# A recurrent gated-memory kernel: GpSimd takes quarter 0's product and half of each cell's hidden rows, under a new order on every engine

## What is computed

```python
encoded = tanh(xt @ We + st @ Ue + be)                                   # 24 values
new_state = tanh(einsum('bd,cds->bcs', xt, Wx) + einsum('bs,cst->bct', st, Ws) + bk)   # 8 candidates of 32
mem = concatenate([[encoded, err]], mem[:-1])                            # the last 20 entries
a = relu(mem.reshape(b, -1) @ enc_w1 + enc_b1)
agent_in = relu(a @ enc_w2 + enc_b2)
h1, c1 = lstm_cell(agent_in, h1, c1, ...)
h2, c2 = lstm_cell(h1, h2, c2, ...)
gate = softmax(h2 @ gate_w + gate_b)
theta = clamp01(mean(abs(mem[:, :10, -1])) * 2.5)
gate = gate * theta + gs * (1 - theta)
st = einsum('bc,bcs->bs', gate, new_state)
pred = clamp01(st[:, -1]); err = pred - yt
```

## Time and profile before

| | us |
|---|---|
| median of 3 runs | 5656.6 (5656.21 to 5656.87) |
| span of the profiled execution | 5654.1 |
| busy: PE, DVE, ACT, POOL | 5444.6, 4678.1, 3830.9, 1646.7 |
| instructions: PE, DVE, ACT, POOL | 67584, 12841, 9217, 3589 |
| DMA, mean | 30 GB/s |

### The profile page before, as it was taken

How to read it: one execution, slowest core, us unless ns; L and a number is a source line. 1 busy time by engine, 2 the same in 40 slices (tenths; PEclk the granted TensorE clock), 3 DMA queues, 4 the chain that set the end, 5 groups by cost and what they waited for, 6 DMA issues and landing times.

```text
span 5654.1 us, 184300 instructions
## 1 busy us (share of the span) xinstructions
PE 5444.6 (96%) x67584; PEld 3397.7 (60%) x67584; DVE 4678.1 (83%) x12841; ACT 3830.9 (68%) x9217; POOL 1646.7 (29%) x3589
## 2 busy tenths in 40 slices
PE   7999999999999999999999999999999999999998
PEld 4666666666666666666666666666666666666665
DVE  7888888888888888888888888888888888888887
ACT  5666666666666666666666666666666666666665
POOL 2222222222222222222222222222222222222222
PEclk9999999999999999999999999999999999999999
DMA  2111111111111111111111111111111111111111
GB/s 66 28 29 30 28 31 28 31 28 31 28 31 28 31 28 28 31 28 31 28 31 28 31 28 31 28 29 30 28 31 28 31 28 31 28 31 28 31 28 39
DMA packets 299286, 172.38 MB, mean 30 GB/s; under 512 B 156734, under 2 KB 263882, under 8 KB 298714
## 3 DMA queue, kind: packets, MB, share of 16 engines
q1 hardware_dynamic: 293568, 159.42, 10.8%
q10 hardware_dynamic: 5146, 3.66, 0.2%
HBM read 74.65 MB, written 2.10 MB: 14 GB/s over the span
## 4 chain that ended last, share of the span: by engine, by line
PE 69%; ACT 15%; DVE 12%; issue 4%; DMA 0%; POOL 0%; ACTq 0%; POOLq 0%; DVEq 0%
PE chain L412 17%; PE a_ps L374 10%; PE cand_ps L343 8%; PE cand_ps L334 8%; ACT a_sb L523 6%; PE chain L399 6%; PE a_ps L363 6%; ACT gates L548 5%; DVE cell_in L708 5%; DVE added L694 4%; PE chain L308 4%; PE a_ps L385 4%; PE chain L429 4%; PE cand_ps L329 3%; ACT tanh_c L554 3%
## 5 line engine op out<-in xcount | busy, mean ns | idle before, releaser
L363 PE MATMUL a_ps<-hist,w_hist 125*64 125x512 f16 x12288 | 1700.2, 381 | 24.9 <-DMA w_hist<-enc_table 24.9
L785 DVE TENSOR_REDUCE state<-mixed 128x64 f32<-128x512 f32 x2048 | 1352.6, 681 | 34.1 <-POOL mixed L873 0.7
L541 ACT ACTIVATE cand<-cand_ps 128x512 f32<-128x512 f32 x2048 | 1154.6, 590 | 184.8 <-PE cand_ps L343 184.8
L412 PE MATMUL chain<-cell_in,cell_w 128*64 128x128 f32 x16384 | 1092.8, 276 | 0.7 <-ACT cell_in L531 0.5
L412 PEld LDWEIGHTS chain<-cell_in,cell_w 128*64 128x64 f32 x16384 | 888.3, 136 | 288.2 <-ACT cell_in L531 181.5
L900 POOL TENSOR_TENSOR err_ring<-pred_now,ys 128x8 f32 x512 | 128.6, 251 | 3106.0 <-DVE pred_now L792 3106.0
L548 ACT ACTIVATE gates<-chain 128x512 f32<-128x512 f32 x1024 | 611.4, 597 | 619.8 <-PE chain L412 619.8
L363 PEld LDWEIGHTS a_ps<-hist,w_hist 125*64 125x64 f16 x12288 | 658.6, 110 | 447.2 <-issue 26.0
L554 ACT ACTIVATE tanh_c<-gates 128x128 f32<-128x128 f32 x1024 | 316.7, 309 | 690.0 <-DVE gates L700 690.0
L694 DVE SCALAR_TENSOR_TENSOR added<-gates 128x256 f32<-128x256 f32 x1024 | 435.5, 425 | 419.4 <-ACT gates L548 419.4
L708 DVE SCALAR_TENSOR_TENSOR cell_in<-gates,tanh_c 64x128 f32<-64x128 f32 x2048 | 588.0, 287 | 159.4 <-ACT tanh_c L554 145.6
(11 more groups left out here) (74 smaller groups left out, 6660.7 us busy)
## 6 DMA issues: line engine op xcount, KB each, us to landing
x_sb<-in_x_l SPq DMA_DIRECT2D x260, 256.0 KB, 2.8
hist<-entry_parts SPq DMA_DIRECT2D x2048, 25.0 KB
w_hist<-enc_table SPq DMA_DIRECT2D x258, 128.0 KB, 2.4
y_rows<-in_y_l SPq DMA_DIRECT2D x260, 8.0 KB
ys<-in_y ACTq DMA_DIRECT2D x1, 2048.0 KB, 16.3
preds_out<-preds SPq DMA_DIRECT2D x1, 2048.0 KB, 8.1
cand<-in_encoder ACTq DMA_DIRECT2D x1, 640.0 KB, 3.8
cell_w<-in_cell ACTq DMA_DIRECT2D x2, 256.0 KB, 4.8
```

Source lines behind the costliest of these rows:

```text
L363: nc.tensor.matmul(a_ps[g][ENC * half:ENC * half + ENC, :], w_hist[0:HROWS, w_slot(u), kk, wp, :], hist[0:HROWS, xp, k, at:at + 512], star ...
L412: last = nc.tensor.matmul(chain[g][rows, P * r:P * r + P], cell_w[c][:, hf, r, :], cell_in[c][:, g, hf, :], start=False, stop=True, skip_g ...
L541: ins = nc.scalar.activation(cand[:, g, q // 2, :, q % 2, :, :].rearrange("p h s c -> p h (s c)"), cand_ps[q][:, :].rearrange("p (h k) -> ...
L785: V.tensor_reduce(state[:, g, hf, 2 * pair:2 * pair + 2, :], mixed[:, pair, hf, :, :, :], AX, ALU.add)\
```

## The change

What it does:

- **GpSimd forms quarter 0's product too.** `mix(pair 0)` is no longer called on VectorE; `mix_quarter` is called for q = 0 and q = 1, each with its own semaphore (`q_mulpool[q]`).
- **Half of each cell's new hidden rows goes to GpSimd**, in two instructions: `out_gate_low` adds 1 to the output gate in 64 rows as soon as the gates are there, and `new_hidden` on GpSimd multiplies with the value's tanh. VectorE keeps the other 64 rows in one instruction. `cell_gates` and `gate_logits` wait for both (`q_h`, `q_h_pool`), and `next_hidden` on ScalarE waits for each half.
- **A semaphore for each sum**: `q_sum[hf][pair]`, waited for one by one.
- **History in one-pass pieces**: `history(item, kk, first, end)` issues single passes, which the new order lays between the other work of TensorE. One of the twelve passes is issued in the item's first phase and eleven in its second.
- **A new order on all compute engines**, and `candidates_x` split in `candidates_bias` (one item ahead) and `candidates_x`. The second encoder layer, the cells and the gate logits of an item are now in its third phase (`old`). `keep_prediction` gets a wait of its own.

The diff, without comments on it and cut to its core:

```diff
-SUMS = 2
-CAND_ORDER = (2, 1, 3, 0)
-MIX_ORDER = (1, 0)
+CAND_ORDER = (3, 2, 1, 0)
+POOL_HALF = (0, 1)
+PIECES = ((0, 0), (1, 0), (0, 1))
...
             def state_transpose(item, hf):
                 g, n, u = item
-                pe.wait_ge(q_sum[hf], SUMS * n)
+                for pair in range(2):
+                    pe.wait_ge(q_sum[hf][pair], n)
...
-            def encoded_x(item, before, extra):
+            def encoded_x(item, extra):
                 g, n, u = item
                 x_wait(item, extra)
-                if before:
-                    for pair in MIX_ORDER:
-                        pe.wait_ge(q_mul[pair], before[1] + GROUPS if pair == MIX_ORDER[1] else before[1])
+                pe.wait_ge(q_mul[1], n)
...
+            def candidates_bias(item):
+                g, n, u = item
+                for q in CAND_ORDER:
+                    pe.wait_ge(q_cand[q], n)
                 for q in range(Q):
                     rows = slice(D_IN * q, D_IN * q + D_IN)
                     nc.tensor.matmul(cand_ps[q][:, :], ones16[rows, :], cand_bias[rows, :],
                                      start=True, stop=False, skip_group_check=True)
...
-            def history(item, kk):
+            def history(item, kk, first=0, end=len(PIECES)):
                 g, n, u = item
                 k = HT - 1 - kk
-                for t, (wp, xp) in enumerate(((0, 0), (1, 0), (0, 1))):
+                for t in range(first, end):
+                    wp, xp = PIECES[t]
...
                     pe.wait_ge(q_h[0], n)
+                    pe.wait_ge(q_h_pool[0], n)
...
                 pe.wait_ge(q_h[1], n)
+                pe.wait_ge(q_h_pool[1], n)
...
 # TensorE, the new order
+                if old:
+                    bias_of_cell(old, 0)
+                    encoder2(old)
+                    candidates_x(old)
+                    cell_gates(old, 0)
+                    candidates_s(old)
+                if cur:
+                    history(cur, 0, 1, 2)
+                if old:
+                    bias_of_cell(old, 1)
+                if cur:
+                    history(cur, 0, 2, 3)
+                    history(cur, 1, 0, 1)
+                    encoded_x(cur, extra)
+                    history(cur, 1, 1, 2)
+                if old:
+                    cell_gates(old, 1)
+                if cur:
+                    history(cur, 1, 2, 3)
+                    state_transpose(cur, 0)
+                    state_transpose(cur, 1)
+                    history(cur, 2, 0, 1)
+                if old:
+                    logit_bias(old)
+                if cur:
+                    history(cur, 2, 1, 2)
                     encoded_s(cur)
+                    history(cur, 2, 2, 3)
                     history(cur, 3)
                 if old:
                     gate_logits(old)
                 if cur:
                     encoder1_now(cur)
                 if new:
+                    history_waits(new, extra)
+                    history(new, 0, 0, 1)
+                if cur:
+                    candidates_bias(cur)
...
 # ScalarE, the new order
+                if cur:
+                    at_least_zero(cur)
+                    encoded(cur)
+                if old:
+                    candidates(old, 0)
+                    exponentials(old)
+                if cur:
+                    encoder1(cur)
+                    entry_high(cur)
+                    agent_input(cur, 0)
+                    agent_input(cur, 1)
+                if old:
+                    next_hidden(old, 1)
+                    next_hidden(old, 0)
                 if cur:
                     cell_tanhs(cur, 0)
+                    candidates(cur, 3)
                     value_tanh(cur, 0)
                     candidates(cur, 2)
                     candidates(cur, 1)
                     cell_tanhs(cur, 1)
                 if new:
                     state_take(new)
                 if cur:
                     value_tanh(cur, 1)
...
 # VectorE, the new order
                 if cur:
+                    error_sum(cur)
+                if old:
+                    totals(old)
+                    reciprocals(old)
+                    shares(old)
+                    fresh_gate(old)
+                    new_gate(old)
+                    mix(old, 1)
                     mix_sum(old, 0, 1)
                     mix_sum(old, 1, 1)
                 if cur:
+                    cell_terms(cur, 0)
+                    cell_value(cur, 0)
+                    thetas(cur)
+                    new_hidden(cur, 0, 1)
+                if old:
+                    mix_sum(old, 0, 0)
+                    mix_sum(old, 1, 0)
+                if cur:
                     cell_terms(cur, 1)
                     cell_value(cur, 1)
+                    new_hidden(cur, 1, 0)
                 if new:
                     errors(new, extra)
+                if old:
+                    prediction(old)
+                if cur:
                     peaks(cur)
                     below_peak(cur)
...
-            def mix_quarter(item):
+            def mix_quarter(item, q):
                 g, n, u = item
                 pool.wait_ge(q_keptfrom, n + GROUPS)
-                pool.wait_ge(q_cand[1], n)
+                pool.wait_ge(q_cand[q], n + 1)
 
                 for hf in range(HF):
-                    pool.wait_ge(q_sum[hf], SUMS * n + SUMS * (GROUPS - 1))
+                    pool.wait_ge(q_sum[hf][0], n + (GROUPS - 1))
...
+            def out_gate_low(item, c):
+                g, n, u = item
+                rows = (CELL0_OUT, CELL1_OUT)[c][POOL_HALF[c]]
+                pool.wait_ge(q_gates[c], n)
+                G.tensor_tensor(out_gate[c][rows, g, :], gates[c][rows, g, 0, :],
+                                ones[rows, 0:1].to_broadcast([HALF, P]), ALU.add).then_inc(q_out[c], 1)
+
+            def new_hidden(item, c, hf):
+                g, n, u = item
+                rows = (CELL0_OUT, CELL1_OUT)[c][hf]
+                pool.wait_ge(q_out[c], n)
+                pool.wait_ge(q_tanhc[c], n)
+                G.tensor_tensor(cell_in[1][rows, g, hf, :], out_gate[c][rows, g, :], tanh_c[c][rows, g, :],
+                                ALU.mult).then_inc(q_h_pool[c], 1)
...
 # GpSimd, the new order
-                if old:
-                    mix_quarter(old)
+                if cur:
+                    kept_gate(cur)
+                    new_hidden(cur, 1, 1)
+                if old:
                     new_error(old, extra)
-                    keep_prediction(old, extra)
-                if cur:
-                    kept_share(cur)
-                    kept_gate(cur)
+                if cur:
+                    gate_in_sbuf(cur)
                 if new:
                     entry_low(new)
                 if cur:
-                    gate_in_sbuf(cur)
+                    mix_quarter(cur, 0)
+                    mix_quarter(cur, 1)
+                if new:
+                    out_gate_low(new, 0)
+                    new_hidden(new, 0, 0)
+                    kept_share(new)
+                if old:
+                    keep_prediction(old, extra)
+                if new:
+                    out_gate_low(new, 1)
```

More of the change, by code:

```diff
@@ L617, in _ @@
             for hf in range(HF):
-                V.memset(state[:, :, hf, :, :], 0.0).then_inc(q_sum[hf], SUMS * GROUPS)
+                for pair in range(2):
+                    V.memset(state[:, :, hf, 2 * pair:2 * pair + 2, :], 0.0).then_inc(q_sum[hf][pair], GROUPS)
             V.memset(share[:, :, :], 0.0).then_inc(s_prep, 1)
@@ L701, in cell_value @@
                                        added[c][:, g, 0, :], ALU.mult, ALU.add).then_inc(q_cell[c], 1)
-            def new_hidden(item, c):
+            def new_hidden(item, c, hf):
                 g, n, u = item
+                rows = (CELL0_OUT, CELL1_OUT)[c][hf]
                 dve.wait_ge(q_tanhc[c], n)
-                for hf in range(HF):
-                    rows = (CELL0_OUT, CELL1_OUT)[c][hf]
-                    last = V.scalar_tensor_tensor(cell_in[1][rows, g, hf, :], gates[c][rows, g, 0, :], 1.0,
-                                                  tanh_c[c][rows, g, :], ALU.add, ALU.mult)
+                last = V.scalar_tensor_tensor(cell_in[1][rows, g, hf, :], gates[c][rows, g, 0, :], 1.0,
+                                              tanh_c[c][rows, g, :], ALU.add, ALU.mult)
                 last.then_inc(q_h[c], 1)
@@ L790, in prediction @@
                 for hf in range(HF):
-                    dve.wait_ge(q_sum[hf], SUMS * n + SUMS * GROUPS)
+                    for pair in range(2):
+                        dve.wait_ge(q_sum[hf][pair], n + GROUPS)
                 V.tensor_scalar(pred_now[:, g, :].rearrange("p (a h l) -> p a h l", a=2, h=HF),
```

139 lines of the change are left out of this document (48 added, 91 removed).

## The result

The changed kernel takes 5816.97 us (median of 4 runs, 5816.65 to 5817.45), the kernel before 5656.54. The ratio is 1.0283, 95% interval 1.0269 to 1.0298: slower by 2.8%, 160 us, or 0.31 us in each of 512 cycles. The forecast was 5790.

What follows compares the result with a forecast made beforehand. TensorE, 96% busy, was taken as bound by its own work in one leg and by latency in three. With cell terms waiting for GpSimd's product, 7.2 + 4.0 = 11.2 us a cycle, times 512 plus 58: 5790 us, range 5490 to 5880.

Steps and rivals of the forecast that it cites:

- rival 1: GpSimd and VectorE don't hold each other up in long instructions: 5498 us, or 5590 if partly shared; chance 0.33 together.
- rival 3: At the second product's end GpSimd's output gate step goes before VectorE's waiting terms: 11.45 us a cycle, 5920 us; chance 0.1.
- the 7.2: Forecast us from the encoder's start to cell 1's logits, through GpSimd's products and cell 0, instead of 6.90 before.
- rows 6: Trace rows before the change: a VectorE cast of 512 columns takes 2.68 us, ending 0.28 after GpSimd's memset.
- Rows 5: Trace rows before the change: small GpSimd and VectorE steps meet and the later waits, none longer than 0.13 us.
- Leg 4: Part of TensorE's cycle from first encoder layer to the next cell 0 logits: 3.15 us before, forecast 3.2.
- leg 1: Part of TensorE's cycle from cell 0's to cell 1's logits: 3.75 us before; TensorE's content forecast 3.55.
- legs 2 and 3: Parts of TensorE's cycle from cell 1's logits over gate logits to encoder: 3.49 and 0.54 us before, together forecast 4.00.
- Theory P: From the experiments: VectorE's two-operand instructions and GpSimd's reads wait for each other, and the chain through the cells pays.
- theory T: From the experiments: the new order, with its switches between shapes of matmuls, has made TensorE's own way longer.
- Rival 2: GpSimd and VectorE wait but hardly meet, products ending 0.3 us earlier: 10.95 us a cycle, 5667 us; chance 0.1.
- Rival 4: On TensorE each single piece costs a 0.1 us matmul switch: 11.1 us a cycle; chance counted within the forecast's 0.47.

Runs made afterwards that it cites:

- small_all: Changed kernel with GpSimd's two products cut to one of 32 state values and its output gate and hidden steps to 8 of 128 columns; output differs: 5652.5 us.
- spare_memsets: Kernel before plus two GpSimd memsets of 128x1400, which only write, behind quarter 1's product: 5661.5 us, ratio 1.0008.
- order_alone: Changed kernel with the old division of work (quarter 0's product and both hidden halves on VectorE), new order and history pieces kept: 5782.3 us.
- small_products: Changed kernel with GpSimd's two products covering one of 32 state values (16 columns instead of 512); output differs: 5761.0 us.
- spare_products: Kernel before plus two unused GpSimd products of 128x512, both operands in SBUF, behind quarter 1's product: 6175.0 us, ratio 1.0915.
- low_later: Changed kernel with GpSimd forming the entry's low half after cell 0's hidden rows instead of before the two products: 6259.2 us.
- the best version: Changed kernel with TensorE reordered, output gate + 1 on ScalarE, entry's low half after cell 0's hidden half, value's tanh before first candidates' tanh: 5549.5 us, ratio 0.981.
- quarter0_back: Changed kernel with quarter 0's product back on VectorE, hidden halves still divided with GpSimd: 5770.2 us.

## Why the prediction was right, point by point

The time, 5817 against 5790, and the sign are right, and the meeting on which they rest took place. But the number owes much to luck. Without long meetings the prediction had 5498 us (rival 1), so it took the change's own gain for 158 us and the meetings' cost for 292. `small_all`, with the meetings taken away, has 5652.5: the gain is 4 us and the cost 164. Two errors of some 150 us and 130 us cancel.

*The legs.* That the cycle splits at the same four points before and after, and that TensorE's work stays the same while its waits move, held; every experiment could be read in these legs.

*GpSimd's queue.* The second product was forecast to end 5.35 us after the encoder's start; it is 2514.56 - 2509.16 = 5.40. The meeting with cell 0's terms is where I put it.

*The price of the meeting.* Terms forecast to end 0.36 after the product: 0.28. The value step 0.16 late: 0.08. GpSimd's hidden half 0.55: 0.49. VectorE did come first, so rival 3 is out. These three were each sized too large: the value step ends 6.09 us after the encoder's start (2515.25), forecast 6.19. Behind the tanh it goes the other way: from its end, 2515.59, to cell 1's logits at 2516.38 are 0.79 us, forecast 0.68, since the logits start 0.15 after GpSimd's half and not 0.05. So the 7.2 is met, at 7.22, by an early and a late part.

*The evidence for it.* The meeting "in large" was read from rows 6, a cast beside a memset. `spare_memsets` shows that a memset of 1.26 us doesn't hold up the terms, so rows 6 are a meeting of another kind and didn't bear on this one; what in the cast makes it wait is not shown. Rows 5, of the kinds of this change, did carry the forecast.

*Leg 4 and TensorE's content.* Leg 4 was taken as 3.2 (bounds 3.15 to 3.3) because ScalarE's chain leaves TensorE room there. It is 3.33, just outside, and `order_alone` has it without any of GpSimd's new work. The x part was sized at 0.86 and its two switches at 0.05 together; it takes 1.08, and the room is 0.93. The same switches make the content of leg 1 3.65 (`small_all`) instead of the 3.55 in the prediction. These two terms were sized wrong. In the prediction's sum leg 4 doesn't count by itself, since cell 0's terms wait for the product's end anyway, so its error doesn't show in 7.2; it shows where the product is out of the way. With legs 2 and 3 at 4.03, forecast 4.0, the cycle is 11.25, forecast 11.2.

*What the loss is made of.* The prediction put all of it on the collisions. The runs say: the new order alone costs 126 us, the new division on top of it 35, and the long products' meeting, on which the forecast rests, 56 (`small_products`). And they say that this is not simply additive: with the moved work all but gone from both engines the new order costs nothing (5652.5), so relieving VectorE is worth up to 130 us to the new order (5782.3 to 5652.5), and GpSimd's waits and lengths take back 164. Theory P explains why the division brings no gain, theory T's leg 4 why the order doesn't, and neither alone gives 160.

*Rivals.* Rival 1 (no long meeting, faster) is refuted by `spare_products`; its time of 5498 would not have come even without meetings: of the 0.31 us a cycle between its 10.62 and `small_all`'s 10.93, leg 4 has 0.13, leg 1 0.10 and legs 2 and 3 0.08. Rival 2 (they hardly meet) falls with the rows above. Rival 4 (switches at every piece) was right for the candidates' lone blocks and wrong for the history passes: in the chain of the kernel after single passes take 0.22, except those ahead of cell 1's bias and of the gate logits' bias, at 0.34. Cell 1's bias itself then takes 0.22 instead of 0.34, so there the two together cost what they did before.

*The DMAs of the entry.* "9 us on" (9.2) and bounds of 0 to 0.1 held for the changed kernel, but the slack was smaller than that sounds: 5.1 us of it are the DMAs' own way, which I hadn't counted, and `low_later` fell into it.

What stays open: how the 164 us of GpSimd's share divide into waits and lengths; what the new order costs in legs 1 and 2 besides leg 4 (0.07 us a cycle in `order_alone`), where only the longer hidden rows were seen; and how much of the best version's gain comes from ScalarE's output gate step, from the place of the low half and from TensorE's order, none of which was run by itself.

## What to carry to other kernels

Before work goes to GpSimd, list the VectorE instructions with two SBUF operands on the chain and the GpSimd instructions that read. Where they overlap the later one waits, and the longer the GpSimd instruction, the longer the wait (0.15 us of terms beside the end of a product here, 1.04 beside a whole one). Work put into a wait of the bound engine is free only while it fits: 0.88 us fitted ahead of cell 0, 1.08 did not. A reordering is checked queue by queue: a producer moved later on one engine stalls whatever stands behind its consumer on another, here the value's tanh behind a candidates' tanh, 0.8 us a cycle. Cutting a cycle into legs between fixed points of the bound engine and reading the same legs in every variant separates causes that the total mixes up.

## What the runs showed of the hardware

- A VectorE instruction with two SBUF operands ended 0.28 us after the end of the GpSimd product that it met, in three kernels (0.28, 0.28, 0.29), whether it had started 0.3 or 1.2 us ahead of that end; beside memsets of the same length it took its usual 0.43 us. Behind a GpSimd step of 64x128 that had started 0.07 before it the distance is the same (0.28, `quarter0_back`).
- A VectorE sum with one operand was not held up beside such a product: 0.69 us, 0.68 elsewhere (`spare_products`).
- A block of 16 candidates' matmuls takes TensorE 0.86 us inside a run of its own shape, 0.97 with a switch behind it and 1.08 alone.
- It goes the other way too: in `small_all`, GpSimd's output gate step on 8 columns took 0.43 us, as long as the terms beside which it starts.
- The way from the end of a GpSimd step over four DMAs on SP's queue to the matmul that waits for them is 5.1 us (`low_later`).
- One cycle in ten of the changed kernel takes 11.37 to 11.40 instead of 11.25 us, at the loop's turn, which the kernel before doesn't show; 51 of them make some 7 us. Its cause was not looked for.
